# A decoder layer with ternary weights: means taken off inside the passes, two sums on ScalarE, one rounding on POOL, a new hand-written order, and a layer that waits for halves

## The chip, the cores and the metric

One core of a Trainium2 chip runs the whole program; the other seven are idle. The metric is the device time of one launch in microseconds (us), the median of several runs. The before and after kernels compute the same function of the same inputs.

## The reference

For 16 sequences of 256 tokens with 256 channels (all f32) one decoder layer is computed:

```python
# 1. recurrent layer with bit-linear projections
def bit_linear(x, w):
    x_scale = clip(max(abs(x), -1), 1e-5)
    x_q = clip(round(x / x_scale * 127), -128, 127)
    w_c = w - mean(w)
    w_scale = clip(mean(abs(w_c)), 1e-5)
    w_q = clip(round(w_c / w_scale), -1, 1)
    return einsum('bsi,oi->bso', x_q, w_q) * (w_scale * x_scale / 127)
h = rms_norm(x, g_pre)
a = sigmoid(bit_linear(h, w_a) + decay_bias)
s = sqrt(clip(1 - a*a, 1e-8)) * sigmoid(bit_linear(h, w_i)) * bit_linear(h, w_v)
rec = chunked_scan(a, s)                     # recurrence over the tokens
attn = x + rec + bit_linear(silu(bit_linear(rms_norm(rec, g_post), w_gate)), w_down)
x = layernorm(x + attn)
# 2. cross attention, 16 heads of 16, rotary turn of q and k, softmax, output projection
x = layernorm(x + xattn(x, ctx))
# 3. a network with weights of +1 and -1
h = s0 * concat([x, -x]) @ W0 ; h = relu(h) * 2      # 1024 wide
h = s1 * h @ W1               ; h = relu(h) * 2      # 1024 wide
x = layernorm(x + s2 * h @ W2)
```

## The kernel before, in words

The unit of work is a group g: one sequence of 256 tokens, two tiles of 128. Sixteen groups (0 to 15) pass through some 90 steps each. Each of the engines has its own list of steps (`steps[...]` in its block), and the order in which an engine takes them is written out by hand: the table `TIMES` gives each step a key per engine (P TensorE, A ScalarE, V VectorE, G POOL, S SyncE, which issues all DMAs), `BEGIN[g]` shifts a group's keys, and `order(engine)` sorts by the sum. The keys decide nothing but the order (and, by the class `Ring`, which PSUM bank an item takes). Three groups are in flight: while group g is in its recurrent layer, g-1 is in attention and g-2 in the +1/-1 network. Engines wait for each other on semaphores only.

Steps with `w:` are the preparation, once, before and among group 0's steps. They matter here:
- Five weights are kept transposed in f32 in `w5s`: w_a, w_i, w_v (512 elements a partition, indices 0 to 2), w_gate and w_down (1024, indices 3 and 4; they lie in the tiles h1h and h1l). DVE sums each (`sums`, L1124), PE adds over the partitions with a matmul by ones (`all_sums`, L819), DVE makes the mean (L1129) and subtracts it from each weight in a pass (`less_mean`, L1132). The sum of magnitudes is then taken on ACT (`magnitudes`, L620; w_a, w_i, w_gate, w_down) and on DVE (w_v, L1137), PE adds again, DVE makes the scale (`spread`, L1141 to L1144) and rounds each weight in three passes (`ternary`, L1147 to L1149).
- POOL builds tables for the rotary turn (`spread` of POOL, L490 and L494), reorders w_k and w_q (`in_order`, L502); PE transposes the tables (L834), ACT copies them (L630). PE also transposes a bias (`value_bias`, L825; ACT L625) and the q and k biases (L842; ACT L635). ACT converts W1 in four pieces (`layer1_weights`, L640), DVE W0 (L1191, L1192) and W2 (L1196).

Steps of a group that matter:
- `scale`: POOL multiplies x by g_pre into xg (L512), ACT sums squares (L646), DVE takes the largest (L1201). `stat1`: POOL takes a root as a power (L516, L518) and makes scales (L526 to L530). `round`: DVE makes the factor (L1214) and rounds xg in two halves (L1207). PE transposes xg (`xqT`, L863), ACT evacuates (L651); then `a`, `aT`, `iv0`, `iv1`, `ivT` on PE (L872, L863), ACT L660, L667, L676, `sq` (L682, L683), DVE `cum` and `recur` (two scans), PE `rec` (L907).
- `rec`, `max2`, `stat2`, `round2`: the same once more on the recurrence's output. ACT L688, DVE L1245, L1246, L1252; POOL `stat2` runs L516, L518, waits for DVE's largest, L539, L540, L543; DVE `round2` is L1260 (two inputs of 128x2, both in SBUF) and L1207 twice (128x256, tensor_scalar). PE's transpose `rqT` (L863) waits for that.
- `rotk`: POOL turns the keys in four full tensor_tensor instructions (L572, L574 twice, L576). `xb`: POOL adds a bias to x1 (L562). `rotq`: DVE L1329, POOL L589 twice, DVE L1331 (both inputs in SBUF). `kp`: parts of k (DVE L1312, L1314, POOL L582).
- attention: `score0` to `score7` (PE L971, DVE reduces each from PSUM, L1345), `max` (L980, L1353, then a DMA of two rows into q_st), `exp` (PE L990, ACT L754), `pv` (PE L1003, ACT L761), `oTok`, `oT`, `wo` (PE L1014, L1022, L1035; DVE L1359, L1360, L1369). DVE's `wo` (L1369) writes x2 and waits for the store of group g-2. `bn2`, `x2`: L1287, L1290, POOL L551, L552, DVE L1295, then `x2T` (PE L1022).
- network: `l0_0` to `l0_3` (PE L1052), each item evacuated by ACT (L779) and DVE (L1389); layer 1 is four items `l1_m` of four parts (PE L1067, 8 matmuls a part, part 0 and 2 read tiles 0 to 3 of h0, part 1 and 3 tiles 4 to 7); layer 2 is `l2.0` to `l2.3` (L1082). Items use two PSUM banks in turn (`ringC`); `take` waits until the bank's former item is evacuated. `l1_0` takes the bank of `l0_2`. Before its part 0, layer 1 waits for all four `l0` items, layer 2 for all four `l1` items.

Of the kernel before, what the change touches and what calls it, by code (L numbers as in the profile page):

```python
# [52 lines left out]
    w:s V-478.88 P-418.9 | w:m V-233.31 A-335.78 P-239.8 | w:a V-140.22 | w:iv V-8.92 | w:g1 V-131.73 P-3.44  # L53
    w:g2 V-12.53 A-10.39 P12.85 | w:gate V35.16 | w:down V39.11 | w:bv P73.77 A78.32 | w:bias P87.08 V99.85
    w:mask V80.1 S-74.71 | w:sgn V47.89 | w:k0 V71.86 | w:k2 V54.66 | w:k1.0 A51.04 | w:k1.1 A57.97 | w:k1.2 A87.6
    w:k1.3 A116.07 | w:rope G22.67 P24.43 A0.45 | w:bqk P39 A49.94 | w:wk G37.27 | w:wq G43.01 | loadx S76.36
    loadc S85.33 | scale A0 G20.62 V21.31 | stat1 G31.46 | round V28.63 | xqT P33.45 A34.05
    iv0 P38.19 A41.31 V43.73 | iv1 P39.93 A46.92 V43.24 | a P35.51 A35.66 | aT P37.8 A38.45 | sq A47.64
    ivT P41.32 V48.52 | cum V49.57 | recur V50.51 | rec P52.46 A57.82 V51.67 | max2 V51.75 | stat2 G72.59
    round2 V52.48 | rqT P64.32 A63.11 | gate0 P65.22 A67.73 V57.36 | gate1 P66.62 A70.4 V58.32 | stat3 G80.11  # L60
    round3 V60.18 | sqT0 P71.7 A73.75 | sqT1 P71.78 A73.93 | down P73.35 V78.28 | bn V79.56 G96.73 | x1 V81.87
    kT P41.81 A55.22 | v P42.7 A66.7 | rotk G78.52 | kp A71.59 V74.64 G94 | kput S76.9 | kget S87.55
    x1T P77.57 A79.34 | xb G126.96 | q P78.85 V84.17 | rotq G122.52 V85.26 | qp A89.4 V90.44 | qput S119.75
    qget S125.36 | score0 P100.6 V104.68 | score1 P106.21 V105.07 | score2 P107.05 V105.17 | score3 P111.4 V105.29
    score4 P116.96 V106.92 | score5 P117.97 V108.75 | score6 P119.32 V108.95 | score7 P121.05 V109.88
    max P123.14 A126.41 V113.54 | maxrow S125.38 | exp0.0 P126.52 A128.77 | exp0.1 P127.1 A129.6 | pv0 P130.22
    exp1.0 P128.98 A129.71 | exp1.1 P129.4 A132.2 | pv1 P131.69 A133.71 | exp2.0 P130.47 A132.27
    exp2.1 P131.23 A133.28 | pv2 P135.49 | exp3.0 P132.11 A133.85 | exp3.1 P132.48 A138.09 | pv3 P138.93 A140.49
    oTok P141.9 V143.37 | oT P144.48 A143.61 | wo P145.37 V144.91 | bn2 V148.17 G179.2 | x2 V154.13
    x2T P148.46 A159.82 V156.33 | l0_0 P149.49 A160.12 V157.13 | l0_1 P150.73 A163.44 V157.83  # L70
    l0_2 P153.11 A163.67 V158.23 | l0_3 P159.04 A164.1 V158.47 | l1_0.0 P161.63 | l1_0.1 P162.94 | l1_0.2 P164.69
    l1_0.3 P166.97 A170.18 V162.36 | l1_1.0 P168.04 | l1_1.1 P171.07 | l1_1.2 P171.65
    l1_1.3 P175.48 A176.62 V164.96 | l1_2.0 P175.63 | l1_2.1 P176.14 | l1_2.2 P177.07
    l1_2.3 P178.43 A185.69 V190.18 | l1_3.0 P178.46 | l1_3.1 P180.22 | l1_3.2 P180.78
    l1_3.3 P182.81 A192.07 V194.21 | l2.0 P196.88 | l2.1 P200.52 | l2.2 P200.69 | l2.3 P200.98 V207.92
    bn3 V232.51 G281.88 | out A248.97 | store S279.54
# [1385 lines left out]
```

## Time and profile before

| what | us |
|---|---|
| median of 3 runs | 925.0 |
| the runs | 924.03, 925.0, 1087.85 |
| the profiled execution | 922.5 |
| its span, first to last instruction | 920.3 |
| PE busy in the span | 814.1 (88%) |
| DVE, ACT, POOL busy | 671.1, 538.4, 277.6 |

The profiled execution has 2.2 us outside its span. All times of rows are us from the start of the span. One matmul of 256 columns starts 0.11 us after the one before it but lasts 0.27 in the rows, since matmuls are pipelined.

### The profile page before, as it was taken

To read this page: it belongs to the slowest core of one execution; us is meant where nothing else is said; L and a number is where in the kernel's file an instruction comes from. 1 tells how busy PE (TensorE), PEld (TensorE's weight loads), DVE (VectorE), ACT (ScalarE), POOL (GpSimd) and SP (SyncE) were. 2 spreads that over 40 slices of the span, in tenths; PEclk is the share of its full clock that TensorE was granted. 3 is DMA by queue.
4 is the path that set the end of the run, shared out by engine and by line. 5 is a ranking of instruction groups with operands and counts; after the bars stand their busy time and mean duration, and the time that the engine had idled before them with its cause. 6 is when DMAs were issued, how large, how long until landed. Compare 5 with 4: busy or idle time off the path is not lost.

```text
span 920.3 us, 17624 instructions
## 1 busy us (share of the span) xinstructions
PE 814.1 (88%) x6731; PEld 640.9 (70%) x6762; DVE 671.1 (73%) x1265; ACT 538.4 (59%) x896; POOL 277.6 (30%) x473
## 2 busy tenths in 40 slices
PE   1655889999999999999999999999999999897966
PEld 1433568786878777787867777777878677775755
DVE  7756578695969687786959696878869596966332
ACT  2635665748484756757484847567574848372421
POOL 6441314142332405151423324051514233221001
...
GB/s 287 0 64 64 41 87 2 127 2 126 13 92 49 59 81 41 100 2 139 2 120 20 88 52 61 79 42 98 3 138 2 120 19 65 53 54 63 1 13 23
DMA packets 52513, 57.42 MB, mean 62 GB/s; under 512 B 7856, under 2 KB 48848, under 8 KB 49360
## 3 DMA queue, kind: packets, MB, share of 16 engines
...
q8 instruction: 54, 0.88, 0.4%
...
## 4 chain that ended last, share of the span: by engine, by line
PE 56%; DVE 22%; ACT 7%; DMA 6%; issue 5%; POOL 3%; SPq 0%; ACTq 0%; DVEq 0%; POOLq 0%
PE bankC L1067 15%; PE bankA L872 7%; PE slotB L990 6%; PE bankA L1003 6%; DVE nmax L1345 6%; PE bankA L937 6%; PE bankA L863 4%; DMA out<-x 4%; PE bankC L1052 4%; DVE h0l L1389 3%; PE bankC L1082 3%; PE slotB L971 2%; PE slotB L1022 2%; DVE st L1260 1%; DVE xg L1207 1%
## 5 line engine op out<-in xcount | busy, mean ns | idle before, releaser
L1067 PE MATMUL bankC<-h0h,w 128*128 128x256 f16 x1024 | 231.1, 272 | 6.6 <-DVE h0l L1389 6.6
L1067 PE MATMUL bankC<-h0l,w 128*128 128x256 f16 x1024 | 230.7, 272 | 0.0
L1345 DVE TENSOR_REDUCE nmax<-slotB 128x4 f32<-128x1024 f32 x128 | 154.1, 1218 | 8.0 <-PE slotB L971 7.0
L754 ACT ACTIVATE pr<-slotB 128x1024 f32<-128x1024 f32 x128 | 128.9, 1031 | 22.1 <-PE slotB L990 21.2
L1067 PEld LDWEIGHTS bankC<-h0h,w 128*128 128x128 f16 x1024 | 99.7, 97 | 22.5 <-issue 9.6
L1067 PEld LDWEIGHTS bankC<-h0l,w 128*128 128x128 f16 x1024 | 100.0, 98 | 11.5
L990 PE MATMUL slotB<-q_st,k_st 99*128 99x256 bf16 x512 | 78.4, 276 | 2.9 <-DMA q_st<-m_lo 2.2
L971 PE MATMUL slotB<-k_st,q_st 97*128 97x256 bf16 x512 | 76.7, 276 | 3.8 <-DVE nmax L1345 2.7
L651 ACT ACTIVATE rqT<-bankA,cst 128x512 bf16<-128x512 f32 x16 | 11.0, 687 | 111.8 <-PE bankA L863 111.8
L551 POOL TENSOR_SCALAR rstd<-mv 128x2 f32<-128x2 f32 x48 | 9.2, 191 | 219.5 <-DVE mv L1290 218.4
L779 ACT ACTIVATE h0h<-bankC 128x512 f16<-128x512 f32 x64 | 38.2, 597 | 60.9 <-PE bankC L1052 60.9
L1003 PE MATMUL bankA<-pr,v_aug 128*32 128x256 f32 x1024 | 65.4, 384 | 0.3 <-ACT pr L754 0.3
L1052 PE MATMUL bankC<-xh,w 128*128 128x256 f16 x256 | 60.2, 278 | 5.0 <-DVE xl L1383 2.9
L990 PEld LDWEIGHTS slotB<-q_st,k_st 99*128 99x128 bf16 x512 | 45.8, 98 | 26.6 <-issue 12.3
L971 PEld LDWEIGHTS slotB<-k_st,q_st 97*128 97x128 bf16 x512 | 49.9, 98 | 19.3 <-DVE nmax L1345 4.4
L1389 DVE SCALAR_TENSOR_TENSOR h1l<-bankC,h1h 128x512 f16<-128x512 f32 x64 | 43.7, 683 | 24.5 <-ACT h1h L779 24.5
L516 POOL TENSOR_SCALAR st<-st 128x2 f32<-128x2 f32 x32 | 6.4, 199 | 181.2 <-ACT junk L688 176.0
L1052 PE MATMUL bankC<-xl,w 128*128 128x256 f16 x256 | 60.0, 277 | 0.0
L1082 PE MATMUL bankC<-w,h1h 128*128 128x256 f16 x256 | 57.6, 272 | 2.2 <-DVE h1l L1389 2.0
L1082 PE MATMUL bankC<-w,h1l 128*128 128x256 f16 x256 | 57.6, 272 | 0.0
L1321 DVE TENSOR_SCALAR qb<-bankA,bcol 128x256 f32<-128x256 f32 x32 | 14.0, 479 | 58.2 <-PE bankA L937 58.2
L589 POOL TENSOR_TENSOR qt<-qb,turn 128x256 f32<-128x256 f32 x32 | 30.7, 977 | 84.5 <-DVE qb L1321 84.5
...
## 6 DMA issues: line engine op xcount, KB each, us to landing
...
```

The lines of the kernel that those rows point to most:

```text
L754: act.activation(pr[i % 2][:, c, :, :].rearrange("p h s -> p (h s)"), slotB[ringB.slot(g, name)][:, :], ACT.Exp, scale=DH ** -0.5).then_in ...
L779: act.activation(flat(dst[:, 2 * m:2 * m + 2, :]), bankC[ringC.slot(g, item)][:, :], ACT.Relu)\
L872: ins = pe.matmul(bankA[ringA.slot(g, name)][:, i * width:(i + 1) * width], xT[:, c, n * P:(n + 1) * P], w[:, c, cols[0]:cols[1]], start=c ...
L937: ins = pe.matmul(bankA[ringA.slot(g, name)][:, e * T:(e + 1) * T], w[:, c, e * P:(e + 1) * P], xT[:, c, :], start=c == 0, stop=c == CT - 1)
L971: ins = pe.matmul(slotB[ringB.slot(g, f"score{un}")][:, j * T:(j + 1) * T], q_st[g % 2][0:K_SCORE, h, n * P:(n + 1) * P], k_st[g % 2][0:K_ ...
L990: ins = pe.matmul(slotB[ringB.slot(g, name)][:, j * T:(j + 1) * T], k_st[g % 2][0:K_SHIFTED, h, c * P:(c + 1) * P], q_st[g % 2][0:K_SHIFTE ...
L1003: ins = pe.matmul(bank[j * VW:(j + 1) * VW, half_:half_ + T], v_aug[g % 2][:, c, i * HG + j, :], pr[i % 2][:, c, j, :], start=c == 0, stop ...
L1052: ins = pe.matmul(bankC[ringC.slot(g, name)][:, e * T:(e + 1) * T], w_0[:, c, (2 * m + e) * P:(2 * m + e + 1) * P], a[:, c, :], start=i == ...
L1067: ins = pe.matmul(bankC[ringC.slot(g, name)][:, e * T:(e + 1) * T], w_1[:, i // 2, (2 * m + e) * P:(2 * m + e + 1) * P], (h0h, h0l)[i % 2] ...
L1082: ins = pe.matmul(bankC[ringC.slot(g, "l2.0")][:, n * D:(n + 1) * D], (h1h, h1l)[i % 2][:, i // 2, n * P:(n + 1) * P], w_2[:, i // 2, :], ...
L1345: dve.tensor_reduce(nmax[:, hg * HG * NT + n:(hg + 1) * HG * NT:NT], slotB[ringB.slot(g, name)][:, :].rearrange("p (h s) -> p h s", s=S), ...
L1389: dve.scalar_tensor_tensor(flat(lo[:, two, :]), bankC[ringC.slot(g, item)][:, :], 0.0, flat(hi[:, two, :]), ALU.max, ALU.subtract).then_in ...
```

## The change

- `less_mean` is gone: `mean` makes the negative mean only. ACT's `magnitudes` add it as the bias of Abs; only w_v still has a pass of its own on DVE. `ternary` has three passes as before, but the first adds the mean and multiplies, the second adds ROUND and takes a maximum, the third a minimum and subtracts.
- The sums of w_gate and w_down (`w:g1`) move from DVE (two L1124) to ACT (Copy with an accumulator), behind `w:m` on ACT.
- The rounding of w_down (`w:down`) moves from DVE to POOL, between `w:wk` and `w:wq`, as three tensor_scalar of 128x1024.
- Layer 1 and layer 2: part 0 waits for the first two items, part 1 for the other two.
- TIMES and BEGIN are new, so the order changes on every engine. Those of weight:
  - PE: `w:bv` and `w:bqk` right around `xqT` of group 0 (before: `w:bqk` between `iv0` and `iv1`, `w:bv` after `down`); in each period `l0_0 l0_1 v score0 l0_2 ... rec l0_3 l1_0.0 score2 score3`, `score5` ahead of `rqT`, `pv1` ahead of `x1T`.
  - ACT in group 0: `kT rec v w:k1.0 w:k1.1 rqT scale#1 gate0` (before: `w:k1.0 scale#1 kT rec w:k1.1 rqT v gate0`); `w:k1.2` ahead of `xqT#1` (before: behind).
  - DVE in group 0: `w:k2` ahead of `ivT`, `w:k0` behind `x1`. In each period `oTok` ahead of `l1_3.3`, and `l1_0.3` and `score4` to `score6` in varying order.
  - POOL in each period, before: `bn2 stat2 xb scale(g+1) rotk`; after: `rotq xb bn2 stat2 rotk scale(g+1)`. So `rotk` comes directly behind `stat2`, and `xb` directly behind `rotq`. For group 15 the order before is `stat2 xb rotk`.
  - SP: `loadx` behind `loadc`, ahead of `kget`.

```diff
+            def down_weights(g):
+                pool.wait_ge(spread_g, 1)
+                w = w5s[4]
+                own.settle(pool.tensor_scalar(w, w, wstat[:, 2, 4:5], wstat[:, 7, 4:5], ALU.add, ALU.mult))
+                own.settle(pool.tensor_scalar(w, w, ROUND, ROUND - 1.0, ALU.add, ALU.max))
+                pool.tensor_scalar(w_down[:, :, :], w.rearrange("p (k n) -> p k n", n=D), ROUND + 1.0, -ROUND,
+                                   ALU.min, ALU.add).then_inc(down_w, 1)
...
             def magnitudes(some, made):
+                act.wait_ge(mean_s, 1 if some[0] == 0 else 2)
                 for n, i in enumerate(some):
-                    act.wait_ge(less, i + 1)
-                    ins = act.activation(spare[n][:, 0:w5s[i].shape[1]], w5s[i], ACT.Abs, accum_out=wstat[:, 3, i:i + 1])
+                    ins = act.activation(spare[n][:, 0:w5s[i].shape[1]], w5s[i], ACT.Abs, bias=wstat[:, 2, i:i + 1],
+                                         accum_out=wstat[:, 3, i:i + 1])
                 ins.then_inc(made, 1)
+
+            def sums(g):
+                act.wait_ge(abs_act, 1)
+                for n, i in enumerate((3, 4)):
+                    act.wait_ge(w_in[i], 16)
+                    ins = act.activation(spare[n], w5s[i], ACT.Copy, accum_out=wstat[:, 0, i:i + 1])
+                ins.then_inc(sum_act, 1)
...
             def layer1(g, m, part):
                 if part == 0:
-                    if m == 0:
-                        for i in range(KT // 2):
-                            pe.wait_ge(*ringC.emptied(g, f"l0_{i}"))
-                        if g == 0:
-                            pe.wait_ge(k1_s, KT // 2)
+                    if m == 0 and g == 0:
+                        pe.wait_ge(k1_s, KT // 2)
                     take(g, ringC, name)
+                if m == 0 and part < 2:
+                    for i in (2 * part, 2 * part + 1):
+                        pe.wait_ge(*ringC.emptied(g, f"l0_{i}"))
...
             def layer2(g, part):
-                    for i in range(KT // 2):
-                        pe.wait_ge(*ringC.emptied(g, f"l1_{i}.0"))
+                if part < 2:
+                    for i in (2 * part, 2 * part + 1):
+                        pe.wait_ge(*ringC.emptied(g, f"l1_{i}.0"))
...
             def ternary(i, dst):
-                own.settle(dve.tensor_scalar(w5s[i], w5s[i], wstat[:, 7, i:i + 1], -1.0, ALU.mult, ALU.max))
-                own.settle(dve.tensor_scalar(w5s[i], w5s[i], 1.0, ROUND, ALU.min, ALU.add))
-                return dve.tensor_scalar(dst, w5s[i].rearrange("p (k n) -> p k n", n=dst.shape[2]), -ROUND, None, ALU.add)
+                w, over = w5s[i], wstat[:, 7, i:i + 1]
+                if i == 2:
+                    own.settle(dve.tensor_scalar(w, w, over, None, ALU.mult))
+                else:
+                    own.settle(dve.tensor_scalar(w, w, wstat[:, 2, i:i + 1], over, ALU.add, ALU.mult))
+                own.settle(dve.tensor_scalar(w, w, ROUND, ROUND - 1.0, ALU.add, ALU.max))
+                return dve.tensor_scalar(dst, w.rearrange("p (k n) -> p k n", n=dst.shape[2]), ROUND + 1.0, -ROUND,
+                                         ALU.min, ALU.add)
```

## Rows read from the trace of the kernel before

**Rows 1.** Busy us (instructions) of PE, PEld, DVE, ACT, POOL in 720 us; clock, DMA share, GB/s
```profile
120.00:840.00 720.00, 687.03 (x5874) 548.51 (x5902) 563.11 (x1065) 456.50 (x765) 223.88 (x385) 1.00 0.32 63
```

**Rows 2.** Waits: engine and line that waited, releaser: us in total, times, longest
```profile
PE bankA L863 <- DVE xg L1207: 13.9, 15, 4.0
...
PE bankC L1067 <- DVE h0l L1389: 6.6, 16, 1.6
...
DVE x L1369 <- DMA out<-x: 12.6, 8, 2.4
```

**Rows 3.** Timeline of the preparation: start, us, engine, line, operation
```profile
7.95 1.82 DVE L1132 TENSOR_SCALAR h0h<-h0h,wstat 128x512 f32<-128x512 f32 x2
...
9.46 1.28 ACT L620 ACT_TABLE_LOAD   x1 [9.46 <-DVE h0h L1132]
...
12.24 0.56 PE L819 MATMUL slotB<-wstat,ones 128*128 128x3 f32 x2 [4.52 <-ACT qpart L620]
...
16.01 2.09 POOL L494 TENSOR_SCALAR kb<-rows 128x256 f32<-128x256 f32 x2
...
18.90 1.06 ACT L620 ACTIVATE kpart<-h1h 128x1024 bf16<-128x1024 f32 x1 [6.80 <-DVE h1h L1132]
...
21.58 1.09 PE L834 MATMUL bankC<-ident,kt 128*128 128x128 f32 x4
...
23.94 1.12 PE L863 MATMUL bankA<-ident,xg 128*128 128x128 f32 x4 [0.41 <-DVE xg L1207]
...
24.09 3.22 POOL L502 TENSOR_SCALAR w_k<-kt 128x256 f32<-128x256 f32 x2
```

**Rows 4.** Timeline, later in group 0: POOL's stat2, a piece of W1, the first scores
```profile
40.90 0.19 POOL L516 TENSOR_SCALAR st<-st 128x2 f32<-128x2 f32 x1 [10.30 <-ACT junk L688]
...
67.57 2.08 ACT L640 ACTIVATE w<-pr,fsc 128x2048 f16<-128x2048 uint8 x1
...
83.35 0.60 PE L971 MATMUL slotB<-k_st,q_st 97*128 97x256 bf16 x4 [1.06 <-DMA q_st<-scr]
```

**Rows 5.** Timeline of round2 in a middle period (group 10): POOL, DVE, PE
```profile
548.14 0.27 POOL L543 TENSOR_SCALAR st<-st,wstat 128x2 f32<-128x2 f32 x1
548.37 1.26 POOL L562 TENSOR_TENSOR x<-x,bo 128x512 f32<-128x512 f32 x1
...
548.63 1.02 DVE L1260 SCALAR_TENSOR_TENSOR st<-st 128x2 f32<-128x2 f32 x1
549.68 0.61 DVE L1207 TENSOR_SCALAR xg<-xg,st 128x256 f32<-128x256 f32 x2
...
550.35 0.66 PE L863 MATMUL bankA<-ident,xg 128*128 128x128 f32 x4 [0.47 <-DVE xg L1207]
```

**Rows 6.** Timeline of round2 of group 15, where rotk follows xb at once
```profile
801.70 1.02 DVE L1260 SCALAR_TENSOR_TENSOR st<-st 128x2 f32<-128x2 f32 x1
...
802.66 1.26 POOL L572 TENSOR_TENSOR kt<-kb,turn 128x512 f32<-128x512 f32 x1
...
802.76 2.05 DVE L1207 TENSOR_SCALAR xg<-xg,st 128x256 f32<-128x256 f32 x2
...
803.88 1.50 POOL L574 TENSOR_TENSOR kt<-kb,turn 128x256 f32<-128x256 f32 x2
```

**Rows 7.** One line's instructions: duration min/median/max in ns, first and last start
```profile
L1260 DVE SCALAR_TENSOR_TENSOR st<-st x16: 161/1023/1029, 43.0 to 801.7; 128x2 f32<-128x2 f32 x16
```

**Rows 8.** Timeline around rotq and oT in a middle period: DVE, then PE
```profile
524.09 0.69 DVE L1331 TENSOR_TENSOR qt<-qt 128x512 f32<-128x512 f32 x1 [1.38 <-POOL qt L589]
...
526.51 0.60 PE L1022 MATMUL slotB<-ident,oN 128*128 128x128 f32 x4
```

**Rows 9.** The end: x2 of group 14; then pieces of the chain that ended last
```profile
837.53 1.59 DVE L1295 TENSOR_SCALAR x<-x,mv,rstd 128x256 f32<-128x256 f32 x2 [1.18 <-POOL rstd L552]
...
893.74 14.15 PE bankC L1067 x128
...
909.49 3.67 PE bankC L1082 x32
```

More of the change, by code:

```diff
@@ L52 @@
 TIMES = """
[L53 to L76, printed above, removed]
+    w:s V-506.5 P-426.93 | w:m V-247.85 A-291.17 P-234.18 | w:a V-183.23 | w:iv V6.37 | w:g1 A-31.29 P-13.34
+    w:g2 V-13.99 A0.08 P1.19 | w:gate V21.58 | w:down G30.99 | w:bv P20.51 A5.17 | w:bias P76.71 V82.98
@@ new lines @@
+    w:mask V69.05 S-93.83 | w:sgn V28.99 | w:k0 V71.65 | w:k2 V34.69 | w:k1.0 A50.93 | w:k1.1 A52.5 | w:k1.2 A73.6
+    w:k1.3 A101.18 | w:rope G1.95 P5.47 A3.64 | w:bqk P22.33 A39.18 | w:wk G16 | w:wq G33.31 | loadx S68.72
+    loadc S64.5 | scale A0 G0.66 V8.88 | stat1 G10.03 | round V18.55 | xqT P21.53 A24.32 | iv0 P27.84 A29.2 V30.09
+    iv1 P28.73 A32.04 V32.59 | a P25.83 A25.36 | aT P27.27 A28.81 | sq A32.91 | ivT P30.5 V35.02 | cum V37.84
+    recur V38.94 | rec P41.21 A45.66 V44.65 | max2 V45.75 | stat2 G49.76 | round2 V46.89 | rqT P49.62 A53.12
@@ new lines @@
+    gate0 P52.93 A53.97 V52.51 | gate1 P53.23 A54.63 V58.44 | stat3 G62.15 | round3 V60.24 | sqT0 P57.6 A65.67
+    sqT1 P58.91 A66.54 | down P59.71 V65.68 | bn V66.38 G67.51 | x1 V70.3 | kT P35.62 A44.12 | v P38.7 A50.38
+    rotk G51.55 | kp A65.4 V65.18 G75.5 | kput S59.58 | kget S70.97 | x1T P67.61 A71.28 | xb G137.82
+    q P71.34 V73.12 | rotq G78.86 V75.97 | qp A78.7 V81.65 | qput S90.71 | qget S97.61 | score0 P93.03 V93.02
+    score1 P94.32 V94.45 | score2 P96.5 V97.85 | score3 P96.87 V99.28 | score4 P100.88 V102.85
@@ new lines @@
+    score5 P102.47 V102.92 | score6 P105.77 V103.05 | score7 P106.76 V104.92 | max P107.27 A114.34 V113.07
+    maxrow S107.58 | exp0.0 P112.14 A120.14 | exp0.1 P117.95 A120.43 | pv0 P119.64 | exp1.0 P118.27 A120.8
+    exp1.1 P119.11 A121.05 | pv1 P120.65 A124.88 | exp2.0 P120.01 A121.96 | exp2.1 P123.67 A125.45 | pv2 P125.65
+    exp3.0 P123.8 A125.47 | exp3.1 P125.06 A127.17 | pv3 P126.53 A130.36 | oTok P128.66 V131.8 | oT P133.28 A132.18
+    wo P134.25 V135.91 | bn2 V136.13 G153.24 | x2 V139.4 | x2T P139.92 A145.07 V141.41
@@ new lines @@
+    l0_0 P142.32 A148.14 V144.65 | l0_1 P144.56 A148.37 V145.24 | l0_2 P146.64 A151.52 V147.1
+    l0_3 P147.57 A151.82 V150.4 | l1_0.0 P149.46 | l1_0.1 P151.47 | l1_0.2 P152.29 | l1_0.3 P153.86 A155.63 V156.04
+    l1_1.0 P154.3 | l1_1.1 P154.91 | l1_1.2 P157.65 | l1_1.3 P160.02 A165.48 V166.08 | l1_2.0 P160.21
+    l1_2.1 P160.25 | l1_2.2 P160.53 | l1_2.3 P160.73 A168.98 V180.66 | l1_3.0 P161.12 | l1_3.1 P165.68
+    l1_3.2 P171.15 | l1_3.3 P171.86 A182.09 V186.61 | l2.0 P185.83 | l2.1 P188.59 | l2.2 P188.92
@@ L77 @@
+    l2.3 P189.29 V192.75 | bn3 V231.84 G235.16 | out A237.5 | store S244.31
 """
-BEGIN = [0, 53.44, 106.92, 160.36, 213.84, 267.29, 320.83, 374.34, 427.93, 481.39, 534.85, 588.3, 641.84, 695.28, 748.81, 802.31]
+BEGIN = [0, 53.19, 106.17, 159.33, 212.45, 265.49, 318.66, 371.69, 424.9, 477.88, 531.06, 584.18, 637.25, 690.47, 743.45, 796.66]
 ENGINES = ("PE", "ACT", "DVE", "POOL", "SP")
@@ L1125, in sums, with mean, mean_iva @@
                 ins.then_inc(sum_asked, 1)
-            def less_mean(k, part, size):
+            def mean(k, part, size):
                 dve.wait_ge(sum_done, 2 * k + 1)
-                own.settle(dve.tensor_scalar(wstat[:, 2, part], sums_p[2 * k][:, 0:part.stop - part.start],
-                                             1.0 / size, None, ALU.mult))
-                for i in range(part.start, part.stop):
-                    dve.tensor_scalar(w5s[i], w5s[i], wstat[:, 2, i:i + 1], None, ALU.subtract).then_inc(less, 1)
-            def less_mean_iva(g):
-                less_mean(0, slice(0, 3), D * D)
-                dve.wait_ge(less, 3)
+                return dve.tensor_scalar(wstat[:, 2, part], sums_p[2 * k][:, 0:part.stop - part.start], -1.0 / size, None,
+                                         ALU.mult)
+            def mean_iva(g):
+                mean(0, slice(0, 3), D * D).then_inc(mean_s, 1)
+                dve.wait_ge(mean_s, 1)
+                own.settle(dve.tensor_scalar(w5s[2], w5s[2], wstat[:, 2, 2:3], None, ALU.add))
                 dve.tensor_reduce(wstat[:, 3, 2:3], w5s[2], AX.X, ALU.add, apply_absolute_value=True).then_inc(abs_asked, 1)
```

37 lines of the change are left out of this document (19 added, 18 removed).

## The prediction

> **What bounds the kernel now.** I read the busy shares first: over the 720 us from 120 to 840 TensorE is busy 687 us at full granted clock, DVE 563, ACT 457, POOL 224 [rows 1]. So PE paces the middle, and only what makes PE wait counts there. The 33 us in which it is idle are 2.3 us a period (a period, one group, is 50.6 us: L1207 of groups 10 and 15 stand at 549.68 and 802.76, [rows 5, 6]). Next the waits of PE: it waited 15 times, 13.9 us in all, for DVE's rounding L1207, and 16 times for the last evacuation before layer 1, 6.6 us [rows 2]. Then the timeline at such a wait. DVE's `round2` begins with L1260, two elements a partition. It takes 0.16 us at best and 1.02 in the median [rows 7]: in the middle period it starts 0.26 us after POOL's L562 and ends as that ends (548.37 + 1.26 = 549.63). Both halves of L1207 follow in 0.61, and PE's `rqT` starts at once, after 0.47 idle [rows 5]. DVE has no gap to speak of in the twenty microseconds before this. So PE is on DVE's heels exactly there, each period, and DVE is held by POOL.
>
> **Preparation.** Read as a chain.
> - ACT can start at the mean (7.91, just ahead of the L1132 row) instead of behind DVE's subtraction: its table load stands at 9.46 [rows 3]. That is 1.5 us earlier; PE's second sum moves from 12.24 to 10.7.
> - DVE loses two sums of 1.2 us and two subtractions of 0.75; ACT takes the sums with one 1.06 + 0.19 each, some 2.2 us overlapped [rows 3], from 10.6 to 12.8. PE and the mean: 13.7. DVE then rounds w_i and w_v (2.7 us, as before) and is at group 0's `round` by 17.3.
> - That is no longer the latest. POOL's tables end at 16.01 + 2.09 = 18.1 [rows 3] and do not move; its root follows (1.05 us), then DVE's factor and rounding (0.8): 20.0. PE must also transpose the tables from 18.1 (two times 1.1), ACT copy them (0.6), and `w:bv` (0.6) is now ahead of `xqT`: 21.6 instead of 23.94 [rows 3]. Gain 2.3.
> - The four transposes of `w:bqk` leave the place between `iv0` and `iv1`: 0.9 more, 3.2 in all.
> - Around `rqT` ACT has two pieces of W1 (2.08 each) ahead of it and `v` no longer behind: I get 0.5 lost. `w:k1.2`, which stood at 67.57 and kept `ya` until 69.55 [rows 4], goes ahead of `xqT#1` into idle time: 0.5 back. W0's and W2's conversions (3.0 and 1.2 on DVE) lie beside PE's q projection (3.75) and ACT's square root (2.0): nothing, and their full length if that cover is gone.
> - Net: the first scores at 80.1 instead of 83.35 [rows 4]. **-3.2.**
> - The unknown is POOL's rounding of w_down, three passes of 1024 elements. From below DVE's 0.75 a pass; from above L502's 1.6 for 256 elements [rows 3], 6.5 a pass. I take the nearest kind, 1.26 for 512 contiguous elements [rows 5], 2.5 a pass, 7.6 us. It starts at about 23.2, `w:wq` (3.3) is queued behind it, then `stat2`, which starts when ACT's squares are done (40.90 now [rows 4], 37.7 then). Slack 37.7 - 23.2 - 3.3 = 11.2, so 7.6 costs nothing and 19.5 costs 8.
>
> **The period: POOL.** `xb` leaves its place behind `stat2`; `rotk`, four full tensor_tensor instructions, takes it. Before, `scale(g+1)` came between, which waits for `rqT` and so for DVE. What the new order does is to be read from group 15, which has no next group: `xb`, then L572 at once. There L1207, ready at 802.76, had to wait for L572, and both halves took 2.05 instead of 0.61 [rows 5, 6]. In the new order L1260 waits for L572 as it did for L562 (no change), then the first half of L1207 for the first L574, the second for the second: `round2` ends at 548.37 + 1.26 + 1.50 + 0.1 = 551.2 instead of 550.29. That is 0.9 later. Bounds: 0, if DVE gets in between POOL's instructions, and 1.44, as in group 15. PE passes it on: `score5` (0.44) now lies ahead of `rqT` and shortens what follows, but score6, score7 and the exponentials hang on DVE's reductions and on the DMA of the maximum, which PE's order leaves as little room as before; so I count 0.9 in full for groups 1 to 14 (group 0 rounds before its `rotk`). 14 x 0.9 = **+12.6**. Group 15 loses `xb` from its chain: **-0.5**.
>
> The Trainium skill, page "SBUF — State Buffer", section "Who interferes with whom", says that DVE and GpSimd share a pair of ports, held for a whole instruction, against DVE instructions with two SBUF inputs or in a two-port mode. The rows of L1260 and L1207 agree. It speaks against this change in a second place, where no row shows it: L1331.
>
> **xb.** It now starts as POOL's L589 ends, the moment that releases L1331 (524.09), whose two inputs are in SBUF like L1260's. If it is held, by 525.25 - 524.09 = 1.16 us. The list behind it has shrunk by `l1_3.3` (0.6), so `oN` comes 0.5 later and PE's `oT`, at 526.51 [rows 8], with it, part of that hidden: DVE's `wo` waited for a store in 8 of 16 groups anyway, 12.6 us [rows 2]. Between 0 and 14 x 0.55 = 7.7 I take **+2**.
>
> **Halves.** In the period PE waited 0.3 to 0.4 for the last `l0` item. The wait goes, but `rqT` comes when DVE lets it: what PE saves lies ahead of a wait on a DVE that has no gap, so it turns into a longer wait at L1207. 0, from below -0.4 x 14 = -5.6. At the end nothing hides it: layer 2 of group 15 starts 909.49 - (893.74 + 14.15) = 1.6 after layer 1 [rows 9], and one part (14.15 / 16 = 0.88) fits in, likewise ahead of layer 1. **-1.8.** And `xb#14` no longer holds DVE's L1295 at 837.5, which took 1.59 instead of 0.74 [rows 9]: **-0.8.**
>
> **Sum**, on the profiled execution (920.3 in the span, 2.2 around it): 922.5 - 3.2 + 12.6 - 0.5 + 2 - 1.8 - 0.8 = 930.8. The median of the runs, 925.0, lies 2.5 above that execution; so **933 us**, 0.9% slower. A measurement of this kernel tells about 2% from no change.
>
> **Rivals.**
> - *The ports cost nothing: faster.* `rotk` comes at a time when DVE does not want the pair, or DVE slips in between L572 and L574, so `round2` stays at 550.3. For it: POOL's sequencer needs a little between instructions, the keys of the new table are shifted (a DVE that arrives 0.5 us before POOL's L543 ends decides for it). Against: `score3` (1.2) still lies between DVE's maximum and L1260, in 14 of 14 groups, and group 15 shows the collision. Then the halves show too: 922.5 - 3.2 - 1.8 - 0.8 - 0.3 x 14 = 912.5, plus 2.5: **915**. Chance 0.33.
> - *Both moves cost in full.* 1.44 a group for `rotk` and 0.55 for `xb`: 922.5 - 5.8 + 20.2 + 7.7 = 944.6, plus 2.5: **947**. Against: the second half finds an L574 of 0.75 only. Chance 0.10.
> - *POOL's rounding is slow.* At L502's rate: +8 on the forecast, **941**. For it: POOL's times vary with form; against: contiguous data. Chance 0.07.
> - *The waits in halves don't do what they say.* `l1_0` takes the bank of `l0_2`, so it waits for three items, not two. Only the last matters, so the time moves by some tenths. No chance of its own.
> - *Everything is better than I see*, with PE's 2.3 us of idle a period falling to 1: 925 - 6 - 18 = 901. Chance 0.05.
>
> **How the numbers follow.** Forecast 0.45, its own range 925 to 943 (0.5 to 1.4 a group). The range that holds 8 in 10 must take in the faster rival, so 909 to 944. Faster by over 2% (under 906.5): 0.05. Slower by over 2% (over 943.5): the second rival and the edge of the third and of the forecast, 0.14. The rest, 0.81, is within 2%.
>
> **What would show it.** In the new profile: L1207 on xg with a mean of about 0.7 instead of 0.35, PE's wait for it up from 13.9 to some 30 us, the distance from L543's end to `rqT` up by 0.9. L1067's wait for L1389 nearly gone. L1331 at 0.7 (xb free) or at 1.8 (held). First scores near 80. POOL's w_down passes at 2.5 each. The forecast is wrong if L1207 keeps 0.35 or if PE's wait at `rqT` doesn't grow while L1207 does.

## The result, and the profile after

The kernel after takes 927.98 us (median of 6 runs, 926.13 to 928.92) beside 923.78 us for the kernel before in the same session: ratio 1.0053 [1.0031, 1.0076]. (One run of the kernel before, 1087.85 us, fell in a slower state of the chip and is left out.) It is slower by half a per cent, well under the 2% by which the prediction tells a change from none, though the interval leaves out 1. The forecast was 933 us with a range of 909 to 944. The profiled execution has a span of 926.0 us against 920.3, and 5.7 us is the sum that the rest of this section breaks up; between the medians it is 4.2 us.

Line numbers have moved: L1207 is now L1229 (rounding), L1260 L1282, L1295 L1317, L1331 L1353, L1369 L1391, L1389 L1411, L863 L878, L1067 L1083, L562 L569, L572 to L576 L579 to L583, L582 L589.

**The middle.** Busy time of each engine from 120 to 840 us (in brackets the instructions), which answers to [rows 1]:

```profile
120.00:840.00 720.00, 683.99 (x5829) 545.70 (x5855) 590.71 (x1052) 458.64 (x761) 227.86 (x382) 1.00 0.31 61
```

VectorE is busy 590.7 us instead of 563.1, though it finishes fewer instructions there (1052 against 1065). Which operations grew is in the groups by line, shapes apart (busy us, mean ns of one | idle time before it), same window; first the kernel before, of which [rows 1] gives only the sum:

```profile
L1295 DVE TENSOR_SCALAR x<-x,mv,rstd 128x256 f32<-128x256 f32 x58 | 22.2, 425 | 23.3 <-POOL rstd L552 23.3
L1207 DVE TENSOR_SCALAR xg<-xg,st 128x256 f32<-128x256 f32 x54 | 18.3, 381 | 1.0
L1260 DVE SCALAR_TENSOR_TENSOR st<-st 128x2 f32<-128x2 f32 x14 | 12.6, 900 | 0.2
```

and the kernel after:

```profile
L1317 DVE TENSOR_SCALAR x<-x,mv,rstd 128x256 f32<-128x256 f32 x56 | 31.2, 598 | 22.3 <-POOL rstd L559 22.3
L1229 DVE TENSOR_SCALAR xg<-xg,st 128x256 f32<-128x256 f32 x54 | 29.2, 581 | 1.0
L1353 DVE TENSOR_TENSOR qt<-qt 128x512 f32<-128x512 f32 x14 | 23.6, 1685 | 9.7 <-POOL qt L596 9.7
L1282 DVE SCALAR_TENSOR_TENSOR st<-st 128x2 f32<-128x2 f32 x14 | 14.4, 1030 | 0.0
```

Three groups are longer by 9 to 14 us each, 34 us together, which is more than the whole growth of 27.6 since the window holds fewer instructions: the rounding, the second step of the rotary turn of q (L1353, 1.69 us on average instead of the 0.69 of [rows 8]), and the normalization (L1317). L1282 was long already. The timeline of `round2` (group 9) shows who is beside them: start, duration, engine, line, and in brackets idle time and its releaser. It answers to [rows 5].

```profile
502.24 0.27 POOL L550 TENSOR_SCALAR st<-st,wstat 128x2 f32<-128x2 f32 x1
502.47 1.27 POOL L579 TENSOR_TENSOR kt<-kb,turn 128x512 f32<-128x512 f32 x1
502.72 1.03 DVE L1282 SCALAR_TENSOR_TENSOR st<-st 128x2 f32<-128x2 f32 x1
...
503.69 1.46 POOL L581 TENSOR_TENSOR kt<-kb,turn 128x256 f32<-128x256 f32 x2
503.79 1.51 DVE L1229 TENSOR_SCALAR xg<-xg,st 128x256 f32<-128x256 f32 x2
...
505.35 0.66 PE L878 MATMUL bankA<-ident,xg 128*128 128x128 f32 x4 [1.28 <-DVE xg L1229]
```

L1282, whose last input POOL had ready at 502.5, ends 0.01 us after POOL's L579 (502.47 + 1.27 = 503.74); L1229's second half ends 0.15 us after L581's second (505.30 against 505.15). TensorE starts 0.05 us after that and had been idle 1.28 us, where [rows 5] had 0.47. A VectorE instruction that is longer because one of POOL runs beside it is called held from here on, and the pair a collision. The same picture stands at two more places of the period:

```profile
520.76 1.16 POOL L589 TENSOR_TENSOR kpart<-krest,kpart 128x512 bf16<-128x512 f32 x1
520.90 1.49 DVE L1317 TENSOR_SCALAR x<-x,mv,rstd 128x256 f32<-128x256 f32 x2 [1.17 <-POOL rstd L559]
...
529.65 1.27 POOL L569 TENSOR_TENSOR x<-x,bo 128x512 f32<-128x512 f32 x1
529.79 1.68 DVE L1353 TENSOR_TENSOR qt<-qt 128x512 f32<-128x512 f32 x1 [0.69 <-POOL qt L596]
```

The second pair is `xb` behind `rotq`, the place [rows 8] was read for. The first was not foreseen: POOL's order had `kp` ahead of `bn`; now `kp` follows `bn`, whose result (L559) is what releases L1317, so the L1317 of this place starts beside L589 in each period (14 times in the window, by the 10.6 us that e3_kp takes off).

**What waited.** Waits of the kernel after (engine, line, tile and what it waited for: us in total, times, longest), beside [rows 2]:

```profile
PE bankA L878 <- DVE xg L1229: 22.2, 16, 4.0
...
DVE x L1391 <- PE slotB L1050: 19.8, 16, 2.9
```

The wait of TensorE for the rounding went from 13.9 to 22.2 us (the prediction had said some 30); the one for the evacuation ahead of layer 1 (6.6 us before) is down to 0.5 us, as the group of L1083 on the page says; VectorE's wait for a store (12.6 us) is gone, since L1391 now waits for TensorE.

**The account of the 5.7 us.** The first scores come at 82.26 us (83.35 in [rows 4]): -1.1. The rounding in `round2` of groups 10 and 15 starts at

```profile
555.38 1.51 DVE L1229 TENSOR_SCALAR xg<-xg,st 128x256 f32<-128x256 f32 x2
...
812.58 1.51 DVE L1229 TENSOR_SCALAR xg<-xg,st 128x256 f32<-128x256 f32 x2
```

5.7 and 9.8 us later than in [rows 5] and [rows 6]; a period there is 51.4 us instead of 50.6. So the 15 periods cost 9.8 + 1.1 = 10.9 us. From `round2` of the last group to the end 4.1 us come back. About half of this is the end of the chain:

```profile
897.82 1.06 PE bankC L1067 x8
...
900.28 14.24 PE bankC L1083 x128
...
916.01 2.79 PE bankC L1099 x24
```

In the kernel before the second l0 step of this chain is 16 matmuls, that is `l0_2` and `l0_3`:

```profile
890.20 1.94 PE bankC L1052 x16
```

Now layer 1 starts as `l0_2` is evacuated and its bank is free (2.46 us after the start of that step instead of 3.54), and the 8 matmuls of `l0_3` lie beside that; likewise only 24 of the 32 matmuls of layer 2 stand behind its wait. From the start of layer 1 to the end of layer 2 it is 916.01 + 2.79 - 900.28 = 18.5 us, where [rows 9] have 909.49 + 3.67 - 893.74 = 19.4.

**The preparation.** Timeline of the kernel after, beside [rows 3]:

```profile
8.06 1.28 ACT L627 ACT_TABLE_LOAD   x1 [8.06 <-DVE wstat L1147]
...
12.51 2.12 POOL L489 TENSOR_SCALAR kt<-rope 128x256 f32<-128x256 f32 x2 [2.90 <-DMA rope<-in_rope]
...
19.03 1.12 PE L849 MATMUL bankC<-ident,kt 128*128 128x128 f32 x4 [2.05 <-POOL kb L493]
...
22.17 1.06 PE L878 MATMUL bankA<-ident,xg 128*128 128x128 f32 x4
...
24.33 1.19 POOL L500 TENSOR_SCALAR h1l<-h1l,wstat 128x1024 f32<-128x1024 f32 x1
25.60 3.65 POOL L501 TENSOR_SCALAR h1l<-h1l 128x1024 f32<-128x1024 f32 x1
29.33 3.64 POOL L502 TENSOR_SCALAR w_down<-h1l 128x1024 bf16<-128x1024 f32 x1
```

ScalarE starts 1.4 us sooner, as expected, and `xqT` of group 0 comes at 22.17 instead of 23.94. Ahead of it TensorE waited for POOL's tables, which end at 19.0, 0.9 later than before. The three passes over w_down take 8.5 us.

### The profile page after: what moved, and what is told of

The parts are those of the page before. It is cut to its first block, busy times and chain, and to the rows that moved or that the text cites. A ratio compares the mean times of both kernels' runs of the same rounds, so it can differ in the third digit from the quotient of the medians.

```text
span 926.0 us, 17624 instructions
## 1 busy us (share of the span) xinstructions
PE 814.4 (88%) x6731; PEld 641.4 (69%) x6762; DVE 703.1 (76%) x1256; ACT 545.3 (59%) x900; POOL 293.5 (32%) x476
## 4 chain that ended last, share of the span: by engine, by line
PE 53%; DVE 25%; issue 7%; ACT 7%; POOL 5%; DMA 2%; SPq 1%; DVEq 0%; ACTq 0%; POOLq 0%
PE bankC L1083 14%; PE bankA L887 6%; PE bankA L952 5%; PE bankA L878 4%; PE bankC L1067 4%; PE slotB L1005 4%; DVE nmax L1367 4%; PE bankC L1099 4%; POOL qt L596 3%; PE slotB L986 3%; DVE qt L1353 3%; PE bankA L1018 3%; DVE xg L1229 2%; PE slotB L1037 2%; DVE st L1282 2%
## 5 line engine op out<-in xcount | busy, mean ns | idle before, releaser
L1083 PE MATMUL bankC<-h0h,w 128*128 128x256 f16 x1024 | 231.2, 273 | 0.6 <-DVE h0l L1411 0.5
L1083 PE MATMUL bankC<-h0l,w 128*128 128x256 f16 x1024 | 230.8, 272 | 0.0
L769 ACT ACTIVATE pr<-slotB 128x1024 f32<-128x1024 f32 x128 | 126.3, 1026 | 21.0 <-PE slotB L1005 20.7
L1083 PEld LDWEIGHTS bankC<-h0h,w 128*128 128x128 f16 x1024 | 100.0, 98 | 13.6 <-DVE h0l L1411 1.2
L1083 PEld LDWEIGHTS bankC<-h0l,w 128*128 128x128 f16 x1024 | 100.1, 98 | 11.6
L794 ACT ACTIVATE h1h<-bankC 128x512 f16<-128x512 f32 x64 | 38.2, 596 | 93.0 <-PE bankC L1083 93.0
L1005 PE MATMUL slotB<-q_st,k_st 99*128 99x256 bf16 x512 | 74.7, 274 | 2.0 <-ACT pr L769 1.3
L986 PEld LDWEIGHTS slotB<-k_st,q_st 97*128 97x128 bf16 x512 | 48.1, 98 | 31.2 <-issue 13.3
L1067 PE MATMUL bankC<-xh,w 128*128 128x256 f16 x256 | 58.5, 273 | 3.6 <-DVE xl L1405 3.0
L1005 PEld LDWEIGHTS slotB<-q_st,k_st 99*128 99x128 bf16 x512 | 46.5, 98 | 21.8 <-issue 9.1
L1067 PE MATMUL bankC<-xl,w 128*128 128x256 f16 x256 | 58.4, 272 | 0.0
L1317 DVE TENSOR_SCALAR x<-x,mv,rstd 128x256 f32<-128x256 f32 x64 | 35.7, 598 | 26.9 <-POOL rstd L559 26.9
L1411 DVE SCALAR_TENSOR_TENSOR h1l<-bankC,h1h 128x512 f16<-128x512 f32 x64 | 43.4, 679 | 13.2 <-ACT h1h L794 13.2
L1411 DVE SCALAR_TENSOR_TENSOR h0l<-bankC,h0h 128x512 f16<-128x512 f32 x64 | 43.7, 683 | 7.4 <-ACT h0h L794 7.0
```

The costliest lines, as they stand in the source:

```text
L769: act.activation(pr[i % 2][:, c, :, :].rearrange("p h s -> p (h s)"), slotB[ringB.slot(g, name)][:, :], ACT.Exp, scale=DH ** -0.5).then_in ...
L794: act.activation(flat(dst[:, 2 * m:2 * m + 2, :]), bankC[ringC.slot(g, item)][:, :], ACT.Relu)\
L986: ins = pe.matmul(slotB[ringB.slot(g, f"score{un}")][:, j * T:(j + 1) * T], q_st[g % 2][0:K_SCORE, h, n * P:(n + 1) * P], k_st[g % 2][0:K_ ...
L1005: ins = pe.matmul(slotB[ringB.slot(g, name)][:, j * T:(j + 1) * T], k_st[g % 2][0:K_SHIFTED, h, c * P:(c + 1) * P], q_st[g % 2][0:K_SHIFTE ...
L1067: ins = pe.matmul(bankC[ringC.slot(g, name)][:, e * T:(e + 1) * T], w_0[:, c, (2 * m + e) * P:(2 * m + e + 1) * P], a[:, c, :], start=i == ...
L1083: ins = pe.matmul(bankC[ringC.slot(g, name)][:, e * T:(e + 1) * T], w_1[:, i // 2, (2 * m + e) * P:(2 * m + e + 1) * P], (h0h, h0l)[i % 2] ...
```

## The experiments

The ratios are to the kernel before, run in the same session on the same chip; its median was 923.4 to 925.0 us, so a difference in us between runs of two sessions is uncertain by one or two us. The experiments on POOL's order change nothing but keys of the table.

**1. e1_rotk, e2_xb, e3_kp, e4_three: the three collisions of the kernel after, taken away one by one and all together.**

```diff
- rotk G51.55            + rotk G54.6      (e1_rotk: behind scale of the next group)
- xb G137.82             + xb G131         (e2_xb: ahead of rotq)
- kp A65.4 V65.18 G75.5  + kp A65.4 V65.18 G66   (e3_kp: ahead of bn)
```

Expected, e1_rotk:

> The changed kernel (928.0) with rotk put back behind scale(g+1) on POOL; all else as changed. Ports theory (DVE's rounding of xg is held by POOL's turn of the keys, 0.9 us a group, and PE waits for it): both halves of the rounding fall from 1.51 to 0.62 and the time falls by 0.6 to 0.9 a group over 14 groups, to 916 to 920. Rival (the order on PE, ACT and DVE makes the new periods longer, the collisions lie beside it): the rounding falls just the same, but the time stays within 2 us of 928.

Measured: 906.21 us, 0.9805 [0.9787, 0.9823]; that is 21.8 us less than the kernel after, and more than any theory had said. The groups by line of e1_rotk, same window:

```profile
L1229 DVE TENSOR_SCALAR xg<-xg,st 128x256 f32<-128x256 f32 x54 | 17.5, 367 | 1.0
...
L1282 DVE SCALAR_TENSOR_TENSOR st<-st 128x2 f32<-128x2 f32 x14 | 3.0, 213 | 0.0
```

and the timeline of `round2`:

```profile
488.15 0.15 DVE L1282 SCALAR_TENSOR_TENSOR st<-st 128x2 f32<-128x2 f32 x1
488.34 0.62 DVE L1229 TENSOR_SCALAR xg<-xg,st 128x256 f32<-128x256 f32 x2
...
490.10 1.27 POOL L519 TENSOR_TENSOR xg<-x,rows 128x512 f32<-128x512 f32 x1 [2.16 <-PE bankA L878]
```

Both operations are free now: `scale` of the next group waits for TensorE's use of xg, so POOL is silent for 2.16 us just when `round2` runs. L1282 is 0.82 us shorter on average and L1229's pair 0.89, 1.71 us a period and 24 us in 14. The median fell by 21.8 us; the span of the profiled execution, the fastest of the four, by 24.3 (926.0 to 901.7). So nine tenths or more of the held time came back. The move also brings `scale` of the next group forward; what that gives is not separated, but it has to fit into the little that the 24 us leave. The expectation had counted the 0.9 us alone: it had taken L1260's 1.02 us as what that operation costs, because it cost that before too.

Expected, e2_xb:

> The changed kernel with xb ahead of rotq instead of behind it. Ports theory: the last step of rotq on DVE falls from 1.68 to 0.69 in 15 groups. It stands ahead of oTok and oT, where PE waited 5.6 us in all; I expect -0.3 a group, 923 to 926. Rival (order on the other engines): no change, 926 to 930.

Measured: 926.85 us, 1.0042 [1.0024, 1.0059]. L1353 is back at 0.69 us (14 us less of VectorE), and the time falls by 1.1 us, which is within the noise of the two ratios (1.0042 and 1.0053). The rival's range, 926 to 930, was the right one.

Expected, e3_kp:

> The changed kernel with kp ahead of bn on POOL, as it was before the change. Ports theory: the normalization of x1 on DVE falls from 1.49 to 0.74 in 15 groups; x1T on PE waited for it 13.7 us in all counting both units, so up to -0.4 a group, 922 to 926. Rival: no change, 926 to 930.

Measured: 925.65 us, 1.0021 [1.0008, 1.0034]. L1317 falls from 598 to 411 ns on average (10.6 us less), the time by 2.3 us, where the intervals just touch. So two of the three collisions are nearly covered in this order; that a collision is there says nothing of its price.

Expected, e4_three:

> All three moves of POOL together. Ports theory: the three collisions are gone, 2.6 us a group of DVE's time; the gains add until another limit is met. 14 x (0.8 + 0.3 + 0.3) = 20 would give 908; a new limit (the store that the residual waits for, which held the old kernel 12.6 us in all) may stop it near 914. Faster than both kernels. Rival: 925 to 928.

Measured: 901.54 us, 0.9762 [0.9748, 0.9777]: faster than both kernels, by 2.4% than the one before, and below the expected 908 since the hold of L1282 is gone as well. It is 4.7 us below e1_rotk, clear of the noise, so the two small collisions together do cost something. Its waits of TensorE from 120 to 840 us show that one for L1229 is left, once in 720 us (16.7 us in the kernel after), and that the longest that remain are those for which the profile shows no releaser (`issue`) and those for ScalarE:

```profile
PE slotB L986 <- issue: 6.4, 12, 1.2
PE bankA L887 <- ACT av L691: 3.2, 13, 0.3
...
PE bankA L878 <- DVE xg L1229: 1.2, 1, 1.2
```

**2. e8_xb_early: does the kernel before pay as well?** There `xb` stands beside L1260 [rows 5].

```diff
- xb G126.96             + xb G175.7       (ahead of rotq of the next group)
```

> The kernel before, with one key of the table changed: xb of the group before goes ahead of rotq instead of behind stat2. Behind stat2 it runs beside L1260, the first DVE operation of round2, which takes 0.90 us on average there and 0.21 us in the run e1_rotk, where nothing of POOL runs beside it. Theory 'a hold on the way from stat2 to xg costs one for one, and the kernel before paid one too': the four or so tenths that L1207 and the rest keep don't change, L1260 falls to about 0.21 us, and 0.7 to 0.8 us a period times 14 comes off: about 913 us, ratio 0.988 or 0.989. Rival 'the hold of L1260 was covered': 922 to 924, ratio 1.00. Rival 'xb ahead of rotq delays rotq and so the scores': 926 or more.

Measured: 913.42 us, 0.9873 [0.9831, 0.9915], 1.3% or 11.7 us less. The groups by line:

```profile
L1260 DVE SCALAR_TENSOR_TENSOR st<-st 128x2 f32<-128x2 f32 x14 | 3.0, 214 | 0.2
```

900 ns have become 214; 14 times the difference is 9.6 us, which the time gives back in full (by its interval it gives 8 to 16 us). The theory stands: an operation on two elements a partition was worth more than 1% of the kernel before.

**3. e10_rotk_alone and e6_pool: the new places of POOL in the kernel before.**

```diff
- rotk G78.52            + rotk G73              (both)
- xb G126.96             + xb G176.5             (e6_pool only: behind rotq)
- kp A71.59 V74.64 G94   + kp A71.59 V74.64 G97  (e6_pool only: behind bn)
```

> The kernel before with one key changed: rotk directly behind stat2, so that xb and scale of the next group come behind it; kp and xb stay otherwise. L1207 should take 1.51 us instead of 0.62 in 14 of the periods, and L1260 stays held, now by rotk. Theory 'the held xg costs one for one': 923.5 + 14 x 0.89 = 936 us, ratio 1.0135, range 1.010 to 1.017. Rival 'rotk alone makes the whole of e6_pool': 946 to 950, ratio 1.025 or more. Rival 'on the order of the kernel before the wait for xg is covered': 923 to 928.

Measured: 930.01 us, 1.0054 [1.0025, 1.0083], so 5.0 us more, not 12.5. L1207 was held as said; of the added wait a part was taken from other waits. TensorE from 120 to 840 us, the kernel before:

```profile
PE bankA L863 <- DVE xg L1207: 7.1, 12, 1.9
PE slotB L1022 <- DVE x L1295: 5.5, 8, 2.1
```

and e10_rotk_alone:

```profile
PE bankA L863 <- DVE xg L1207: 16.4, 12, 1.4
...
PE slotB L1022 <- DVE x L1295: 3.1, 7, 0.5
```

9.3 us more at the rounding, 2.4 less at L1295 (and 0.7 less at the transposes of iv, further down the list). Taking away 1.71 us a period in the kernel after (e1_rotk) gave nine tenths back; adding 0.89 a period here, where other waits shrink for it, cost 40% of it.

> The kernel before with only POOL's places of rotk, xb and kp as in the changed kernel. Ports theory: the three DVE groups grow as they did in the changed kernel (0.62 to 1.51, 0.69 to 1.68, 0.74 to 1.49) and the time grows by 0.7 to 1.2 a group, to 934 to 941: more than the whole change, whose other parts then give something back. Rival (the other orders are what costs): within 2 us of 924.

Measured: 948.86 us, 1.0283 [1.0251, 1.0314], above both. The two further moves, worth 1 and 2 us in the kernel after, cost 19 us here (21 by the ratios). In the window they lengthen L1331 by 13.9 us in sum and L1295 by 7.5, and TensorE from 120 to 840 us shows a wait that the kernel before has not:

```profile
PE bankA L863 <- DVE xg L1207: 16.4, 12, 1.4
PE bankC L1082 <- DVE h1l L1389: 13.1, 13, 1.1
```

So POOL's new order, put into the kernel before, costs 25 us. The kernel after pays 4: the rest of the change gives 21 back.

**4. e5_halves, e9_pool_halves, e11_undivided, e12_three_undiv: is it the halves?** In e5 and e9 the new functions of layer 1 and layer 2 go into the kernel before and into e6_pool; in e11 and e12 the old ones go into the kernel after and into e4_three.

```diff
  def layer1(g, m, part):
-     if part == 0 and m == 0:
-         for i in range(KT // 2):
-             pe.wait_ge(*ringC.emptied(g, f"l0_{i}"))
+     if m == 0 and part < 2:
+         for i in (2 * part, 2 * part + 1):
+             pe.wait_ge(*ringC.emptied(g, f"l0_{i}"))
```

> The kernel before with only the waits in halves for layers 1 and 2. My reading: at the end 1.8 us are saved; in the periods the saved wait (0.4) turns into a longer wait for the rounding on DVE, so nothing. Ratio to before 0.998, 922.0 from 923.8. Rival (PE-bound periods: 0.3 to 0.4 a group are kept): 0.992, 916 to 918.

Measured: 920.86 us, 0.9974 [0.9956, 0.9992]: 2.6 us less, as expected, and its chain ends like that of the kernel after, with 24 matmuls of layer 2:

```profile
906.17 2.79 PE bankC L1084 x24
```

> The run e6_pool (the kernel before with POOL in the order of the kernel after, 948.9 us) with the halves of layer 1 and layer 2 added. In e6_pool the second half of layer 1 (L1082) waited 13.1 us in the matmul and 16.3 us ahead of the weight load for h1l of L1389, which in the kernel before it does not. Theory 'POOL's places cost what two held operations cost (some 13 us), and the rest of e6_pool's excess is the undivided layer that then waits for VectorE, which halves take away': 930 to 937 us, ratio 1.007 to 1.015. Rival 'halves are worth the 2.6 us of e5_halves everywhere': 946 us, ratio 1.025. Rival 'the order on the other engines is what makes the kernel after faster than e6_pool': also 944 to 948.

Measured: 955.07 us, 1.0316 [1.0264, 1.0368]. The theory fell: halves give nothing in e6_pool; the time is 3 us longer by the ratios, with intervals that overlap. The wait for h1l is gone, and the same time stands elsewhere, still behind VectorE:

```profile
PE bankA L863 <- DVE xg L1209: 20.7, 13, 2.0
PE slotB L1022 <- DVE oN L1362: 13.0, 14, 1.2
```

What is left is the order of TensorE, ScalarE and VectorE (and the preparation), with or without the halves.

> The kernel after with layer 1 and layer 2 of the network as in the kernel before: each waits for all four items ahead of its first part. The run e9_pool_halves has shown that halves are not what takes the kernel after from e6_pool's 948.9 us to 928.0. Theory 'halves are worth what e5_halves showed, mostly at the end, and the 21 us come from the order on TensorE, ScalarE and VectorE': 929 to 932 us, ratio 1.006 to 1.010. Rival 'in the order of the kernel after, where layer 1 begins sooner behind l0_3, halves are worth much more': each of 14 periods would show a wait of the matmuls of layer 1 for h0l or h0h of 0.5 us or more, and the time would be 935 to 945 us. Rival 'nothing at all': 928 us.

Measured: 968.46 us, 1.0473 [1.0439, 1.0507]. Halves are worth 40.5 us in the kernel after (39 by the ratios), of the kind that the rival had said but more. Waits of TensorE from 120 to 840 us in e11_undivided:

```profile
PE bankC L1097 <- DVE h1l L1409: 25.2, 13, 2.0
PE bankC L1082 <- DVE h0l L1409: 24.6, 14, 1.8
```

and its timeline at one of them:

```profile
512.76 0.27 PE L1067 MATMUL bankC<-xl,w 128*128 128x256 f16 x1
514.79 0.27 PE L1082 MATMUL bankC<-h0h,w 128*128 128x256 f16 x1 [1.76 <-DVE h0l L1409]
```

The new order puts part 0 of `l1_0` directly behind `l0_3`, where `rec`, `score1` and `score2` stood between. With the old wait TensorE stands 1.8 us there for the evacuation of the item that it has just finished. Layer 2 keeps its place, but VectorE's new order has `oTok` ahead of the evacuation of `l1_3.3`, and the old wait of layer 2 is for that evacuation too (L1097, 25.2 us). The two waits add 49.8 us; against them the wait for the rounding has gone from 16.7 us to 2.5, since a TensorE that comes later finds xg ready. In the kernel after, the same two instructions follow without a gap:

```profile
496.80 0.27 PE L1067 MATMUL bankC<-xl,w 128*128 128x256 f16 x1
496.91 0.27 PE L1083 MATMUL bankC<-h0h,w 128*128 128x256 f16 x1
```

since part 0 needs only items 0 and 1 and the bank of item 2, and by part 1, 1.75 us later with `score2` and `score3` between, item 3 is evacuated.

> The kernel e4_three (rotk behind scale, xb ahead of rotq, kp ahead of bn on POOL; 901.5 us) with layer 1 and layer 2 undivided as in the kernel before. Its counterpart on the other side is e8_xb_early (913.4 us), the kernel before with no POOL instruction beside L1260 and L1207 either; between the two lie the preparation, the order on TensorE, ScalarE and VectorE, and nothing else. Theory 'halves give some 2 to 3 us, at the end': 903.5 to 905 us, ratio 0.978 to 0.981, so that order and preparation keep 8 to 10 of the 12 us between e8_xb_early and e4_three. Rival 'with VectorE's debts gone TensorE is bound by its own work, and a whole layer's wait costs in each period': 908 us or more.

Measured: 948.25 us, 1.0259 [1.0233, 1.0285]: 46.7 us for the halves in e4_three. The theory is out; the rival, a wait in each period, holds (L1082 waits 24.6 us and L1097 20.1), but its "908 or more" had named no such size.

**5. e7_down: w_down rounded on VectorE again, as in the kernel before.**

```diff
- w:down G30.99          + w:down V21.6    (three passes, ternary() of VectorE)
```

> The changed kernel with the rounding of w_down on DVE again, behind that of w_gate. Its three passes on POOL took 8.5 us and pushed w_q's reordering onto DVE's scan of group 0 (1.61 instead of 1.25). If that is what took most of the missing 2 us of the preparation: scan back near 1.25, first scores 0.5 to 1.0 earlier than 82.26, total 927.0 to 927.5. Rival (it costs nothing, DVE's own 2.7 us then delay something): 928 to 929.

Measured: 927.57 us, 1.0048 [1.0033, 1.0063]. 8.5 us of POOL or 2.6 of VectorE, and no difference in the time: this part of the change is hidden either way. The first scores come at 81.27 instead of 82.26, and that microsecond is lost again further on.

## Why the prediction was right, and where it was wrong

**Right: the direction, the place and most of the size.** `rotk` behind `stat2` makes L1229 run beside L581. Forecast +0.9 us a period; measured 1.51 - 0.62 = 0.89 us, and TensorE's idle time before `rqT` went from 0.47 to 1.28. Fifteen periods cost 10.9 us; the terms for them were 12.6 + 2 = 14.6 us. The main rival, that the ports cost nothing, is out: at all four places the VectorE operation is longer by 0.75 to 1.0 us, where POOL's instruction beside it had 1.0 to 1.4 us left to run (L1317: 520.76 + 1.16 - 520.90 = 1.02 left, 0.75 longer; L1353: 1.13 left, 0.99 longer; L1229 beside the two of L581: 1.36 left, 0.89 longer). The rule of the Trainium skill, page "SBUF — State Buffer", section "Who interferes with whom", thus held at the place where no row had shown it: L1353, with two SBUF inputs, takes 1.69 us instead of 0.69. That the pair is held for a whole instruction does not hold for every POOL instruction of this trace. In the preparation L1209, which also reads two inputs in SBUF, started 0.67 us into L501, which had 2.98 us left, and took 0.39 us, where it takes 0.16 in e7_down:

```profile
26.27 0.39 DVE L1209 TENSOR_TENSOR fsc<-fsc,svec 128x1 f32<-128x1 f32 x1
```

So a hold for about all that POOL's instruction has left is shown here for instructions of 0.7 to 1.3 us only; why this slow one holds less stays open. The signs that the prediction named came out so: the way from L550's end to `rqT` grew by 0.9 us (1.94 to 2.84), L1353 is held, and layer 1's wait is nearly gone; the mean of L1229 is 0.58 and not 0.7, the wait for it 22.2 and not 30, and the first scores come at 82.26 and not near 80.

**Right by cancelling: the middle.** That a held microsecond costs a microsecond is too simple. In the order of the kernel before the same move costs 5 us (e10_rotk_alone), and the two small ones 19 (e6_pool); in the order of the kernel after their removal gives 22 (with L1282's hold, which the kernel before paid too), 1 and 2. The step "PE passes it on, so I count 0.9 in full" holds for the kernel after, by e1_rotk. The step on `xb`, "between 0 and 7.7 I take +2", was sound: 1.1 us, not clear of the noise.

**Wrong: the halves.** The step was "what PE saves lies ahead of a wait on a DVE that has no gap, so it turns into a longer wait at L1207. 0", and -1.8 at the end. The end is right (18.5 us instead of 19.4 from layer 1 to the end of layer 2, and a microsecond more ahead of it), and for the kernel before so is the whole (e5_halves, -2.6 us). But halves and order were costed apart. The new order of TensorE has `rec l0_3 l1_0.0`, and the prediction didn't ask what that would cost without the halves: 40 us. The new order without halves is a loss: some 20 us with POOL's collisions in both (e11_undivided against e6_pool), 35 without them in either (e12_three_undiv against e8_xb_early). The halves without it are 2.6 us or nothing. Together they bring 21 us with the collisions (927.98 against 948.86) and 10 to 12 without (901.54 against 913.42). That is what makes POOL's loss nearly vanish. In these numbers "order" takes in the preparation too.

How far the forecast was lucky depends on the way one goes from one kernel to the other. It put POOL's moves at 13.3 us (12.6 + 2 - 0.5 - 0.8) and the rest at -5.0 (-3.2 - 1.8). By way of e6_pool POOL's moves cost 25 and the rest gave back 21: two errors that cancel. By way of the two kernels without these collisions, e8_xb_early and e4_three, the collisions cost 12 us before the change and 26 after it, 14 to 15 more, close to what was forecast, and the rest gave 10 to 12. On either way the term that was far too small is the rest.

**Missed: `kp` behind `bn`.** No step of the prediction costs it, though the new keys show it. It holds L1317 by 0.75 us a period and costs 2.3 us (e3_kp, where the intervals just touch).

**Too large: the preparation, -3.2 forecast, -1.1 measured.** ScalarE's earlier start is right. The step that failed is "POOL's tables end at 16.01 + 2.09 = 18.1 and do not move": they end at 19.0, since the passes of its table builder are slower; the first took 1.77 us in the kernel before and takes 2.12 in the one after (what stands beside them on VectorE has changed, but no run isolates that; in e7_down the first took 1.83, the other two as long as here, and the tables ended at 19.1):

```profile
12.40 1.77 POOL L490 TENSOR_SCALAR kt<-rope 128x256 f32<-128x256 f32 x2 [3.30 <-DMA rope<-in_rope]
```

`xqT` came at 22.17, not 21.6. POOL's w_down took 8.5 us, not 7.6, and was hidden as the step says, but `w:wq` was pushed to 32.94, beside VectorE's scan of group 0. With 8.5 us taken off POOL (e7_down) that scan takes 1.23 us again instead of 1.60, the first scores come 1 us sooner, and the end does not. Of the 2.1 us that are missing, 0.6 are there at `xqT` and 1.0 goes with w_down; the last 0.5 is open.

**Right: the last group.** -0.5 for `xb` off the chain and -0.8 for L1295 of group 14: L1317 takes 0.74 us there (at 847.29) instead of 1.59 [rows 9]. With the halves' 1.8 (2.0 by the two chains) this makes 3.1 us, of the 4.1 that come back.

**What stays open.** Why the held L1331 and L1295 cost almost all of their 21 us in the order of the kernel before, and 3.4 of 24 us in that of the kernel after, was not taken apart further: the waits show only that TensorE is on VectorE's heels in several places of the one (e6_pool, e9_pool_halves) and in one of the other. And e1_rotk, e2_xb and e3_kp give 25.2 us one by one, e4_three 26.4 together, so there the effects add.
